# Copies of x moved from SyncE's queue to ScalarE's, and a reordered hand-over in a gated expert layer

## The chip, the cores and the metric

The kernel runs on one core of one Trainium2 chip. The metric is the device time of one execution in microseconds (us). The core has five engines, each with its own in-order instruction stream: TensorE (PE; its weight loads are shown apart as PEld), VectorE (DVE), ScalarE (ACT), GpSimd (POOL) and SyncE (SP, which here only begins DMAs). They meet through semaphores. DMAs begun by SyncE, ScalarE and GpSimd go through one queue each (q1, q10, q0 in the profile) and are carried out by the same 16 DMA engines.

## The reference

```python
W = weights[condition]                          # 64 of 16 matrices 64 x 64
y = einsum('bct,bcd->bdt', x, W)                # x: 64 x 64 x 1024, so 4096 rows ("tokens") of 1024
logits = y @ W_gate + b_gate                    # 8 experts
_, top_idx = top_k(logits, 2)
y_all = relu(einsum('bsd,edh->bseh', y, W_e) + b_e)   # W_e: 8 x 1024 x 1024
out = x + take_along_axis(y_all, top_idx[..., None], axis=2).mean(axis=2)
```

All is float32. Each token adds half of the relu of two experts' rows to its own row of x.

## The kernel before

**Two stages.** In the first, 32 tiles of 128 tokens are loaded, multiplied by their condition matrices on TensorE, copied from PSUM by ScalarE and stored in DRAM (y_rows); VectorE turns them for the gate. Tokens are dealt with in NG = 8 groups of 512 tokens. For group g VectorE chooses the two experts (choose), works out each token's place in its expert's list (slots), TensorE adds up the lists (fill) and VectorE writes them to SBUF (list_out). SyncE writes them to a table in DRAM, one slot per routed token, with eight small DMAs (table_out, L328).

In the second stage each tile is 128 slots of one expert: GpSimd gathers their rows of y (L471 for ordinary tiles, L457 for early ones), VectorE turns them, ScalarE casts them to a rounded high part (a_hi), VectorE subtracts it for the low part (a_lo), and TensorE does three products (high x high, high x low, low x high) at line 613, 48 matmul instructions a tile. VectorE adds the bias (finish, L1002), ScalarE does the relu (L731), and GpSimd adds the rows to out with a scatter that accumulates (L488 for early tiles, L500 for the others). There are 69 tiles.

**Early tiles.** Expert 0's first seven tiles (EARLY = 7, numbered 0 to 6) start before the table is complete: early tile t needs only tokens of the first t + 1 groups. SyncE reads its 128 slots back as soon as group t is in the table (read_first, L314, four DMAs), VectorE makes row numbers of them (read_from, L981), GpSimd gathers (early), VectorE turns (turn_early, L1018), ScalarE casts (early_hi, L737), VectorE subtracts (early_lo, L1023). TensorE does the products of early tiles 0 to 6 in order, with the gate work of groups 4 to 7 put between them by hand (hooks).

**From the table on.** Once all groups are in it, ScalarE loads the whole table to SBUF with four DMAs (L778), VectorE rearranges it in six kinds of instruction (L1096 to L1106) and makes the row numbers of all slots; GpSimd can then gather tile 7 and those after it, which are the ordinary tiles. schedule() works out which expert each tile belongs to. After the last early tile has been split (s_alo at EARLY) SyncE loads expert 1's bias and weights, which ScalarE and VectorE split into high and low parts (L726, L884).

**Copies.** out must hold x before results are added to it. The last four tiles are stored from SBUF; for the rest 14 copies of 1 MB go from x to out in DRAM (copy, L343), begun by SyncE and never more than two in flight: copy c waits for copy c - 2, with two semaphores in turn. scatter_early(t) waits for copies 2t and 2t + 1.

**What sets the order.** No planner does: every engine's stream is written out by hand. SyncE's tail reads: bias, copies 0 and 1, pad row block, table_out(4), copies 2 and 3, read_first(4), table_out(5), copy 4, read_first(5), copy 5, table_out(6), copy 6, read_first(6), copy 7, table_out(7), copies 8 to 13, and then bias and weights of expert 1. VectorE's tail is the straight list after its loop over 32 tiles, beginning with choose(LATE): it ends with read_from(6), schedule, early_out, finish_early(3), turn_early(5), early_lo(5), the table, finish_early(4), turn_early(6), early_lo(6), finish_early(5), and then tile 7.

Of the kernel before, what the change touches and what calls it, by code (L numbers as in the profile page):

```python
# [27 lines left out]
def build(nc, x, itok, cond_w, gate_w, gate_b, exp_w, exp_b, out, y_dram, table):  # L28
# [46 lines left out]
    with ExitStack() as ctx:  # L75
# [6 lines left out]
        def sem(name):  # L82
            return ctx.enter_context(nc.semaphore(name))
# [140 lines left out]
        s_copy = [sem(f"s_copy{i}") for i in range(2)]  # L224
# [74 lines left out]
        with nc.Block() as block:  # L299

            @block.sync
            def _(sp):
# [7 lines left out]
                def read_first(t):  # L310

                    sp.wait_ge(s_sc[t], LAND)
                    for q in range(Q):
                        sp.dma_start(first[q * R:(q + 1) * R, t, :], slots_by[:, t, :]).then_inc(s_first[t], 16)  # L314
# [24 lines left out]
                def copy(c):  # L339
                    if c >= 2:  # L340
                        sp.wait_ge(s_copy[c % 2], c // 2 * 16)
                    at = slice(left[c] * P, (left[c] + 2) * P)
                    sp.dma_start(out[at, :].rearrange("(o r) d -> r o d", o=2),  # L343
                                 x_rows[at, :].rearrange("(o r) d -> r o d", o=2)).then_inc(s_copy[c % 2], 16)

# [17 lines left out]
                sp.wait_ge(s_y, NTILE - 2)  # L363
                copy(0)
                copy(1)

                sp.dma_start(out[TOK:TOK + P, :], x_rows[0:P, :]).then_inc(s_pad, 16)
                table_out(LATE)
                copy(2)
                copy(3)  # L370
                read_first(4)
                table_out(LATE + 1)
                copy(4)
                read_first(5)
                copy(5)
                table_out(LATE + 2)
                copy(6)
                read_first(6)
                copy(7)
                table_out(LATE + 3)  # L380
                for c in range(8, len(left)):
                    copy(c)
# [26 lines left out]
            def _(pool):  # L409
# [70 lines left out]
                def scatter_early(t):  # L480

                    for j in range(2):
                        pool.wait_ge(s_copy[j], (t + 1) * 16)
                    if t:
                        pool.wait_ge(s_add, t * 16)
                    pool.wait_ge(s_out, t + 1)
                    pool.wait_ge(s_to, t + 1)
                    pool.indirect_dma_start(  # L488
                        out=out, out_offset=bass.IndirectOffsetOnAxis(ap=first_to[:, t:t + 1], axis=0),
                        in_=out_of(tile(0, t)), in_offset=None, compute_op=ALU.add).then_inc(s_add, 16)  # L490
# [193 lines left out]
            def _(act):  # L684
# [59 lines left out]

                conditions(0)
# [6 lines left out]
                for n in range(NTILE):  # L752
# [9 lines left out]
                    if n == NTILE - 4:  # L762
                        early_hi(0)
                early_hi(1)
                logits_out(NG - 2)
                relu(tile(0, 0))
                early_hi(2)
                logits_out(NG - 1)
                relu(tile(0, 1))
                early_hi(3)  # L770
                early_hi(4)
                relu(tile(0, 2))
                for g in range(NG):
                    act.wait_ge(s_sc[g], LAND)
                act.wait_ge(s_yout[0], 16 * NG)
                act.wait_ge(s_turn, NTILE)
                for q in range(Q):
                    act.dma_start(ys[q * R:(q + 1) * R, 0, :].rearrange("p (b w) -> p b w", w=P).bitcast(U32),  # L778
                                  slots_all).then_inc(s_tab, 16)
# [45 lines left out]
            def _(dve):  # L825
# [257 lines left out]
                turn_early(4)  # L1083
                early_lo(4)
                list_out(NG - 1)
                read_from(6)
# [4 lines left out]
                early_lo(5)  # L1091

# [17 lines left out]
                finish_early(4)  # L1110
                turn_early(6)
                early_lo(6)
# [83 lines left out]
```

## Time and profile before

| | us |
|---|---|
| median of 3 runs (lowest, highest) | 889.76 (889.64, 892.01) |
| the profiled execution | 886.84 |
| its span | 885.2 |
| PE busy | 849.0 (96%) |
| PEld busy | 672.8 (76%) |
| DVE busy | 428.8 (48%) |
| POOL busy | 447.3 (51%) |
| ACT busy | 257.0 (29%) |

The profile is of one execution; its times count from the start of its span. Busy shares are means over the whole span: the stretch in which the change lies is 100 to 210 us, where one stage hands over to the other. A row of a timeline gives start, length, engine, line, operation, written tile, read tiles, how many instructions are taken together, and in brackets the idle time of the engine before it and who ended it. Rows of SPq, ACTq and POOLq are the issuing of a DMA; the transfer itself comes after, and "landing" is the time from issue until all of it has arrived.

### The profile page before, as it was taken

To read this page: it belongs to the slowest core of one execution; us is meant where nothing else is said; L and a number is where in the kernel's file an instruction comes from. 1 tells how busy PE (TensorE), PEld (TensorE's weight loads), DVE (VectorE), ACT (ScalarE), POOL (GpSimd) and SP (SyncE) were. 2 spreads that over 40 slices of the span, in tenths; PEclk is the share of its full clock that TensorE was granted. 3 is DMA by queue.
4 is the path that set the end of the run, shared out by engine and by line. 5 is a ranking of instruction groups with operands and counts; after the bars stand their busy time and mean duration, and the time that the engine had idled before them with its cause. 6 is when DMAs were issued, how large, how long until landed. Compare 5 with 4: busy or idle time off the path is not lost.

```text
span 885.2 us, 16693 instructions
## 1 busy us (share of the span) xinstructions
PE 849.0 (96%) x4154; PEld 672.8 (76%) x4155; DVE 428.8 (48%) x578; ACT 257.0 (29%) x310; POOL 447.3 (51%) x500
## 2 busy tenths in 40 slices
PE   8788999899999999999999999999999999999993
PEld 4444577777888888888888888888888888888883
DVE  6698777656643373335533363336333733333320
ACT  5656411034421151114211331115111511111220
POOL 3002324267566667654665556555655465555311
PEclk9899999999999999999999999999999999999997
DMA  9999987998965695447754495546654565444433
GB/s 337 417 417 360 332 301 221 313 327 269 295 132 110 120 298 121 101 95 201 196 107 91 106 289 102 111 99 217 171 109 99 186 119 106 89 101 99 80 48 47
DMA packets 51034, 162.47 MB, mean 184 GB/s; under 512 B 11594, under 2 KB 11658, under 8 KB 50986
## 3 DMA queue, kind: packets, MB, share of 16 engines
q0 software_dynamic: 24544, 76.74, 40.0%
q1 hardware_dynamic: 20618, 67.79, 21.0%
q10 hardware_dynamic: 5840, 17.57, 5.0%
q8 instruction: 14, 0.23, 0.1%
q14 instruction: 18, 0.15, 0.0%
HBM read 106.74 MB, written 70.52 MB: 200 GB/s over the span
## 4 chain that ended last, share of the span: by engine, by line
PE 82%; DMA 6%; DVE 5%; issue 2%; ACT 2%; SPq 1%; ACTq 0%; POOL 0%; DVEq 0%; POOLq 0%
PE psO L613 79%; DMA y_rows<-ys 1%; DMA raw<-in_L_ffn_W_e 1%; DVE turned L864 1%; PE psO L554 1%; ACT ys L707 1%; DMA ys<-slot_table 1%; DMA first<-slot_table 1%; DMA slot_table<-lists 1%; DMA raw<-in_L_cond_weights 1%; SPq L328 1%; PE psG L566 0%; DVE w_lo L877 0%; DVE bias L1018 0%; SPq L325 0%
## 5 line engine op out<-in xcount | busy, mean ns | idle before, releaser
L613 PE MATMUL psO<-w_hi,a_hi 128*128 (+1 forms) x1104 | 342.6, 392 | 4.5 <-DVE a_lo L1023 3.5
L613 PE MATMUL psO<-w_hi,a_lo 128*128 (+1 forms) x1104 | 340.6, 390 | 0.0
L613 PE MATMUL psO<-w_lo,a_hi 128*128 (+1 forms) x1104 | 340.5, 390 | 0.0
L471 POOL DMA_INDIRECT rows<-y_rows,idx_g x248 | 255.5, 1030 | 106.7 <-issue 51.5
L613 PEld LDWEIGHTS psO<-w_hi,a_hi 128*128 128x128 f32 x1104 | 206.6, 188 | 49.3 <-DVE a_lo L1023 4.4
L613 PEld LDWEIGHTS psO<-w_lo,a_hi 128*128 128x128 f32 x1104 | 207.6, 188 | 43.3
L613 PEld LDWEIGHTS psO<-w_hi,a_lo 128*128 128x128 f32 x1104 | 207.6, 188 | 43.3
L1040 DVE TENSOR_TENSOR a_lo<-ys,a_hi 128x1024 fp32r<-128x1024 f32 x62 | 75.9, 1225 | 113.4 <-ACT a_hi L743 113.4
L731 ACT ACTIVATE ys<-ys 128x1024 f32<-128x1024 f32 x33 | 35.0, 1061 | 262.4 <-DVE ys L1002 262.4
L731 ACT ACTIVATE rows<-rows 128x1024 f32<-128x1024 f32 x33 | 35.0, 1060 | 249.7 <-DVE rows L1002 249.7
L1002 DVE TENSOR_TENSOR ys<-psO,bias 128x1024 f32<-128x1024 f32 x33 | 40.3, 1222 | 123.2 <-PE psO L613 91.9
L1002 DVE TENSOR_TENSOR rows<-psO,bias 128x1024 f32<-128x1024 f32 x33 | 40.4, 1223 | 112.4 <-PE psO L613 76.6
L1029 DVE STREAM_TRANSPOSE ys<-rows 128x1024 f32<-128x1024 f32 x62 | 76.7, 1237 | 14.1 <-DMA rows<-y_rows,idx_g 14.1
L884 DVE TENSOR_TENSOR w_lo<-raw,w_hi 128x1024 f32 x56 | 65.3, 1222 | 36.1 <-ACT w_hi L726 35.9
L500 POOL DMA_INDIRECT out<-rows,idx_s x31 | 55.2, 1781 | 40.2 <-issue 17.4
L500 POOL DMA_INDIRECT out<-ys,idx_s x31 | 53.6, 1730 | 37.7 <-ACT ys L731 18.3
L467 POOL COPY idx_g<-idx_all 128x4 uint32 x62 | 26.5, 427 | 87.3 <-issue 59.8
L743 ACT CAST a_hi<-ys 128x1024 fp32r<-128x1024 f32 x62 | 64.9, 1047 | 12.7 <-issue 9.8
L457 POOL DMA_INDIRECT raw<-y_rows,from_q x28 | 29.3, 1045 | 71.8 <-DVEq L982 51.3
L726 ACT CAST w_hi<-raw 128x1024 f32 x56 | 55.2, 1048 | 7.1 <-DMA raw<-in_L_ffn_W_e 5.9
L864 DVE STREAM_TRANSPOSE turned<-ys 128x1024 f32<-128x1024 f32 x32 | 39.4, 1239 | 14.0 <-ACT ys L707 11.9
L707 ACT COPY ys<-psO 128x1024 f32<-128x1024 f32 x32 | 32.4, 1012 | 21.0 <-PE psO L554 14.0
(141 smaller groups left out, 333.3 us busy)
## 6 DMA issues: line engine op xcount, KB each, us to landing
raw<-in_L_ffn_W_e SPq DMA_DIRECT2D x56, 512.0 KB, 5.9
y_rows<-ys ACTq DMA_DIRECT2D x32, 512.0 KB, 8.7
out<-in_x SPq DMA_DIRECT2D x14, 1024.0 KB, 6.4
rows<-in_x SPq DMA_DIRECT2D x16, 512.0 KB, 10.5
more_x<-in_x SPq DMA_DIRECT2D x16, 512.0 KB, 10.4
bias<-in_L_ffn_b_e SPq DMA_DIRECT2D x8, 512.0 KB, 7.1
rows<-y_rows,idx_g POOLq DMA_INDIRECT x248
raw<-in_L_ffn_W_e POOLq DMA_DIRECT2D x4, 512.0 KB, 9.1
```

What stands on the lines that cost most here:

```text
L471: pool.indirect_dma_start(out=rows[:, slot, a * DQ:(a + 1) * DQ], out_offset=None, in_=y_parts[0:(1 + TOK) * Q, :], in_offset=bass.Indirec ...
L500: pool.indirect_dma_start(out=out, out_offset=bass.IndirectOffsetOnAxis(ap=idx_s[:, m:m + 1], axis=0), in_=o_sb[m], in_offset=None, comput ...
L613: last = nc.tensor.matmul(ps[:, h * BANK:(h + 1) * BANK], a[:, p, k * P:(k + 1) * P], w[:, bass.ds(slot + (k * H + h * BANK), BANK)], star ...
L707: nc.scalar.copy(ys[:, s, :].rearrange("p (q k j) -> p q k j", q=Q, k=KD), psO[n % 2][:, :].rearrange("p (k q j) -> p q k j", q=Q, k=KD)). ...
L726: nc.scalar.copy(w_hi[:, bass.ds(at, H)], raw[:, k, :]).then_inc(s_hi, 1)
L731: nc.scalar.activation(out_of(t), out_of(t), ACTF.Relu, scale=0.5).then_inc(s_out, 1)
L743: nc.scalar.copy(a_hi[:, m % 2, :], ys[:, m % 2, :]).then_inc(s_ahi, 1)
L864: V.transpose(turned[:, g % 2, :, s * R:(s + 1) * R], ys[:, s, :].rearrange("p (b i) -> p b i", i=R)).then_inc(s_turn, 1)
L884: V.tensor_tensor(w_lo[:, bass.ds(at, H)], raw[:, k, :], w_hi[:, bass.ds(at, H)], ALU.subtract).then_inc(s_split, 1)
L1002: V.tensor_tensor(out_of(t), psO[m % 2][:, :], bias[:, bass.ds((e % 2) * H, H)], ALU.add).then_inc(s_bo, 1)
L1029: V.transpose(ys[:, p, :].rearrange("p (k a i) -> p k a i", k=KD, a=Q), rows[:, p, :].rearrange("p (a k j) -> p k a j", k=KD, a=Q)).then_i ...
L1040: V.tensor_tensor(a_lo[:, p, :], ys[:, p, :], a_hi[:, p, :], ALU.subtract).then_inc(s_alo, 1)
```

## The change

SyncE begins no copies any more, so nothing on it waits for one. It writes lists 4 to 7, reads the slots of early tiles 4 to 6 each after its own list, and then begins the load of the whole table in ScalarE's place. ScalarE begins all 14 copies in five batches between its other work, waits for none, and each copy has a semaphore of its own. On VectorE read_from(6) goes from behind list_out(7) to ahead of early_lo(4), and finish_early(4), turn_early(6), early_lo(6) go from behind the work on the table to ahead of the wait for it.

```diff
-        s_copy = [sem(f"s_copy{i}") for i in range(2)]
+        s_copy = [sem(f"s_copy{i}") for i in range((NTILE - G) // 2)]
@@ SyncE
-                def copy(c):
-                    if c >= 2:
-                        sp.wait_ge(s_copy[c % 2], c // 2 * 16)
-                    at = slice(left[c] * P, (left[c] + 2) * P)
-                    sp.dma_start(out[at, :].rearrange("(o r) d -> r o d", o=2),
-                                 x_rows[at, :].rearrange("(o r) d -> r o d", o=2)).then_inc(s_copy[c % 2], 16)
-
...
                 load_bias(0)
-                sp.wait_ge(s_y, NTILE - 2)
-                copy(0)
-                copy(1)
 
                 sp.dma_start(out[TOK:TOK + P, :], x_rows[0:P, :]).then_inc(s_pad, 16)
-                table_out(LATE)
-                copy(2)
-                copy(3)
-                read_first(4)
-                table_out(LATE + 1)
-                copy(4)
-                read_first(5)
-                copy(5)
-                table_out(LATE + 2)
-                copy(6)
-                read_first(6)
-                copy(7)
-                table_out(LATE + 3)
-                for c in range(8, len(left)):
-                    copy(c)
+                for g in range(LATE, NG - 1):
+                    table_out(g)
+                    read_first(g)
+                table_out(NG - 1)
+
+                for g in range(NG):
+                    sp.wait_ge(s_sc[g], LAND)
+                sp.wait_ge(s_yout[0], 16 * NG)
+                sp.wait_ge(s_turn, NTILE)
+                for q in range(Q):
+                    sp.dma_start(ys[q * R:(q + 1) * R, 0, :].rearrange("p (b w) -> p b w", w=P).bitcast(U32),
+                                 slots_all).then_inc(s_tab, 16)
                 sp.wait_ge(s_alo, EARLY)
@@ GpSimd
-                        pool.wait_ge(s_copy[j], (t + 1) * 16)
+                        pool.wait_ge(s_copy[2 * t + j], 16)
@@ ScalarE
+                def copies(lo, hi):
+
+                    for c in range(lo, hi):
+                        at = slice(left[c] * P, (left[c] + 2) * P)
+                        act.dma_start(out[at, :].rearrange("(o r) d -> r o d", o=2),
+                                      x_rows[at, :].rearrange("(o r) d -> r o d", o=2)).then_inc(s_copy[c], 16)
+
...
                         early_hi(0)
+                copies(0, 3)
                 early_hi(1)
                 logits_out(NG - 2)
+                copies(3, 5)
                 relu(tile(0, 0))
                 early_hi(2)
+                copies(5, 7)
                 logits_out(NG - 1)
+                copies(7, 9)
                 relu(tile(0, 1))
                 early_hi(3)
+                copies(9, 12)
                 early_hi(4)
                 relu(tile(0, 2))
-                for g in range(NG):
-                    act.wait_ge(s_sc[g], LAND)
-                act.wait_ge(s_yout[0], 16 * NG)
-                act.wait_ge(s_turn, NTILE)
-                for q in range(Q):
-                    act.dma_start(ys[q * R:(q + 1) * R, 0, :].rearrange("p (b w) -> p b w", w=P).bitcast(U32),
-                                  slots_all).then_inc(s_tab, 16)
+                copies(12, len(left))
                 relu(tile(0, 3))
@@ VectorE
                 turn_early(4)
+                read_from(6)
                 early_lo(4)
                 list_out(NG - 1)
-                read_from(6)
                 schedule()
                 early_out(4, EARLY)
                 finish_early(3)
                 turn_early(5)
                 early_lo(5)
+                finish_early(4)
+                turn_early(6)
+                early_lo(6)
 
                 dve.wait_ge(s_tab, Q * 16)
...
                 dve.sem_inc(s_idx, 1)
-                finish_early(4)
-                turn_early(6)
-                early_lo(6)
                 finish_early(5)
```

## Rows read from the trace of the kernel before

**Rows 1.** The page, part 5: product group, its busy time and waiting
```profile
L613 PE MATMUL psO<-w_hi,a_hi 128*128 (+1 forms) x1104 | 342.6, 392 | 4.5 <-DVE a_lo L1023 3.5
```

**Rows 2.** Chain that ended last, in order of time: start, length, what
```profile
207.08 109.09 PE psO L613 x480
316.31 555.18 PE psO L613 x2448
```

**Rows 3.** Timeline of TensorE, 150 to 215 us
```profile
167.22 0.61 PE L613 MATMUL psO<-w_hi,a_lo 128*128 128x512 f32 x2
170.53 0.73 PE L613 MATMUL psO<-w_hi,a_hi 128*128 128x512 f32 x2 [2.70 <-DVE a_lo L1023]
...
184.15 0.73 PE L613 MATMUL psO<-w_hi,a_hi 128*128 128x512 f32 x2 [0.81 <-DVE a_lo L1023]
...
195.17 0.61 PE L613 MATMUL psO<-w_hi,a_hi 128*128 x2
...
207.08 0.72 PE L613 MATMUL psO<-w_hi,a_hi 128*128 x2 [0.88 <-DVE a_lo L1040]
```

**Rows 4.** Windows: length, busy PE PEld DVE ACT POOL, PEclk, DMA share, GB/s
```profile
171.00:174.00 3.00, 3.00 (x11) 2.35 (x10) 1.26 (x2) 0.00 (x0) 0.00 (x0) 0.64 1.03 285
174.00:177.00 3.00, 3.00 (x12) 2.41 (x11) 2.79 (x4) 0.00 (x0) 0.00 (x0) 0.79 1.01 414
```

**Rows 5.** Timeline of VectorE, 95 to 215 us
```profile
152.81 1.23 DVE L1023 TENSOR_TENSOR a_lo<-bias,a_hi 128x1024 fp32r<-128x1024 f32 x1 [1.11 <-ACT a_hi L737]
...
154.30 0.21 DVE L947 TENSOR_TENSOR lists<-list_high,psL 64x64 uint32<-64x64 f32 x1
158.00 0.23 DVE L981 TENSOR_SCALAR from_q<-first,part_q 128x4 uint32<-128x4 uint32 x1 [3.49 <-DMA first<-slot_table]
...
169.25 1.22 DVE L1023 TENSOR_TENSOR a_lo<-bias,a_hi 128x1024 fp32r<-128x1024 f32 x1 [1.11 <-ACT a_hi L737]
172.71 1.11 DVE L1096 COPY ys<-ys 128x1024 uint32<-128x1024 uint32 x1 [2.23 <-DMA ys<-slot_table]
...
179.32 1.23 DVE L1002 TENSOR_TENSOR rows<-psO,bias 128x1024 f32<-128x1024 f32 x1 [0.22 <-DVE idx_row L996]
...
182.82 1.27 DVE L1023 TENSOR_TENSOR a_lo<-bias,a_hi 128x1024 fp32r<-128x1024 f32 x1 [1.12 <-ACT a_hi L737]
...
187.90 1.25 DVE L1029 STREAM_TRANSPOSE ys<-rows 128x1024 f32<-128x1024 f32 x1 [2.67 <-DMA rows<-y_rows,idx_g]
190.31 1.26 DVE L1040 TENSOR_TENSOR a_lo<-ys,a_hi 128x1024 fp32r<-128x1024 f32 x1 [1.16 <-ACT a_hi L743]
...
201.05 1.24 DVE L1029 STREAM_TRANSPOSE ys<-rows 128x1024 f32<-128x1024 f32 x1
...
205.46 1.23 DVE L1040 TENSOR_TENSOR a_lo<-ys,a_hi 128x1024 fp32r<-128x1024 f32 x1 [2.06 <-ACT a_hi L743]
```

**Rows 6.** Timeline of GpSimd: last of the four gathers for tile 7
```profile
182.48 0.95 POOL L471 DMA_INDIRECT rows<-y_rows,idx_g  x1 [0.30 <-issue]
```

**Rows 7.** Timeline of SyncE: the issuing of DMAs
```profile
148.71 0.58 SPq L343 DMA_DIRECT2D out<-in_x  x1
151.39 1.73 SPq L314 DMA_DIRECT2D first<-slot_table  x4
...
159.37 20.39 SPq L343 DMA_DIRECT2D out<-in_x  x6
```

**Rows 8.** Landing of read_first: all, then those issued 151 to 153.2 us
```profile
DMA to landing us min/median/max: 1.7/5.5/8.0
...
first<-slot_table SPq DMA_DIRECT2D x4, 0.5 KB, 4.5
```

**Rows 9.** Issue of DMAs: table load by ScalarE, and all copies by SyncE
```profile
162.38 1.77 ACTq L778 DMA_DIRECT2D ys<-slot_table  x4
...
L343 SPq DMA_DIRECT2D out<-in_x x14: 572/580/1832, 104.8 to 179.2; - x14
```

**Rows 10.** Timeline of ScalarE: cast of early tile 1
```profile
110.62 1.05 ACT L737 CAST a_hi<-bias 128x1024 fp32r<-128x1024 f32 x1 [5.31 <-DVE bias L1018]
```

## The prediction

> **What bounds the kernel now.** I read the page first. Its fifth part puts the three products of line 613 at some 343 us each and gives their engine 4.5 us of waiting in all, 3.5 of it for the low halves of early tiles (L1023) [rows 1]. The chain of waits then shows where it could move: from 207.08 us to 871.49 there is nothing but TensorE on the products [rows 2]. After 207 us TensorE never waits. So the question is only when the product of tile 8 (the second ordinary tile) starts, 207.08 now. An edit that moves this start moves the end by as much; one that doesn't is worth nothing.
>
> The TensorE timeline shows the holes ahead of it [rows 3]: 2.70 us before early tile 5 (170.53), 0.81 before early tile 6 (184.15), none before tile 7 (195.17), 0.88 before tile 8. After the hole of 2.70 us the granted clock is 0.64 in 171 to 174 and 0.79 in 174 to 177 [rows 4], the lower of the two levels (1.2 GHz) for part of each, while PE is fully busy. In work that is 3.0 x 0.36 + 3.0 x 0.21 = 1.7 us. The 0.8 us holes were followed by no fall. All that can be won is 2.70 + 1.7 + 0.81 + 0.88 = 6.1 us.
>
> Why they are there, by VectorE's timeline [rows 5]: it runs strictly in order. At 154.51 it has written list 7, then idles 3.49 us for the read of early tile 6's slots (158.00), then does schedule and turns early tile 5; its low half ends at 170.47, and TensorE starts 0.06 later. Then 2.23 us of waiting for the whole table (172.71), some 6.5 us of work on it, and only then tile 6.
>
> **The change part by part.**
> 1. read_from(6) moves ahead of early_lo(4) and list_out(7). This is the edit that speaks against the change: the instruction waits for a DMA, and behind it stand the low half of early tile 4, which TensorE wants at about 167.83 - 10.95 = 156.9 (the last product of tile 4 ends at 167.83, [rows 3], and a tile takes 184.15 to 195.17, some 11.0), and list 7, from which the table comes. Call F the moment at which the read of tile 6 is there: 158.00 now. The low half then ends at F + 0.35 + 1.23 and list 7 at F + 2.05, where both were done by 154.51.
> 2. All behind it on VectorE follows F. From 158.00 to the end of early tile 5's low half are 12.47 us [rows 5]; the two moved items add 154.51 - 152.81 = 1.70. So tile 5 starts at F + 12.47 + 1.70 + 0.06 = F + 14.2. Break-even against 170.53 is F = 156.3.
> 3. finish_early(4), turn_early(6), early_lo(6) come ahead of the table. They took 179.32 to 184.09 [rows 5], 4.8 us: tile 6 is ready at F + 19.0, while TensorE needs it only at F + 25.2. The 0.81 hole goes, for sure.
> 4. The price is paid by the table: its work starts at S = F + 19.0 instead of 172.71. From there to the end of tile 7's low half it took 191.57 - 172.71 = 18.86 [rows 5], so F + 37.8. In it lie 4.47 us between GpSimd's last gather issue (ends 183.43) and the turn (187.90) [rows 5, 6], beside the copies (issued to 179.76 [rows 7]); a small read was back in as little as 1.7 [rows 8]. I let it come between 2 and 4.5: F + 35.3 to F + 37.8. TensorE is there after two tiles, F + 14.2 + 22.0 = F + 36.2. Tile 7 so starts at F + 36.2 to F + 37.9; I take F + 36.6.
> 5. Bias and weights of expert 1 are begun by SyncE when early tile 6 is split (s_alo at 7), so at F + 19 instead of 184.1. The weights were the cause that VectorE turned tile 8 only at 201.05; from that turn to the end of the low half are 5.64 us [rows 5]. Now they lie ready: four splits of 1.2 us after tile 7's low half, the turn, and 5.64 come to some 10.5 to 11 us after it, against the 10.95 that tile 7 keeps TensorE busy. Hole 0 to 0.5, taken 0.2 instead of 0.88. **Tile 8 starts at F + 36.6 + 10.95 + 0.2 = F + 47.8**, against 207.08 now.
> 6. SyncE: table_out and read_first no longer stand behind copies' waits, and it begins the table's loads (four issues took ScalarE 1.77 us [rows 9]). It is idle otherwise. The table took 172.71 - 154.51 = 18.2 us from list to landing; S allows it F + 19.0 - (F + 2.05) = 17.0. It needs to be 1.2 us quicker, and the copies that ran beside it (six from 159.37 to 179.76 [rows 7]) are by then all begun: the last go out after relu of tile 2, some 154 to 157 us. I count it as in time; if it isn't, 1.2 us.
> 7. ScalarE issues 14 copies. One issue was 0.57 to 1.83 us on SyncE [rows 9]: at most 3 x 1.83 = 5.5 for the batch of three. The first batch stands ahead of 5.31 us of idle time before the cast of early tile 1 [rows 10]; the other batches stand ahead of such waits too. Cost 0; if the cover were gone in one place, 0.5 to 2 us, and it would have to be made up in front of list 4 to 7.
> 8. Separate semaphores: scatter_early(t) waits for the same copies as before, all of them earlier. 0.
>
> **What F is.** Before, the four reads are issued in 151.39 to 153.12, right behind a 1 MB copy issued on the same queue at 148.71 [rows 7], and their median landing is 4.5 us after issue [rows 8]. The issue time stays: it is set by TensorE's count for list 6 and the landing of its writes. After, no copy stands ahead in SyncE's queue, but up to three (begun at 141 or later) are in ScalarE's, and the adding scatter of early tile 1 in GpSimd's. Bounds for the landing from the reads' own row: 1.7 and 8.0, so F = 154.8 to 161.1. I take 157.3, near to the same read before (158.0) with a little off for the copy that no longer stands in front: the scatter remains.
>
> The Trainium skill (DMA: Bandwidth & Descriptors, section Queues, rings and completion order) says that each DMA engine takes the queues that have work for it in turn, a packet from each; by that the read passes a backlog in another queue. The same page, under Issuing engines are not separate DMA queues, says that starting DMAs from several engines saves only the issue time. By the first F would fall, by the second it would stay at 158.0 and the table would be no quicker. No row of before has such a read beside copies in the other queue alone; the second is a rival below.
>
> **Sum.** F = 157.3 gives a start of tile 8 at 205.1, 2.0 us sooner. The profiled execution took 886.84 us (span 885.2 and 1.6 around it), so 884.8 for such an execution; it lies 2.9 under the median of the runs, 889.76, so for a median 887.8. What a measurement here can tell from no change is about 0.3%, 2.7 us. By steps: hole 5 with its slow clock becomes a smaller hole before tile 4 (F + 1.7 - 156.9 = 2.1) and one of 1.5 before tile 5. Should the clock fall after the first, tile 4 runs 1.7 longer inside that second hole and nothing is lost; should it fall after the second, up to 1.4 is.
>
> **Rivals.**
> - *The read is back much sooner* (F = 154.8 to 156.6). For it: nothing in front on its queue, and a landing of 1.7 is on the row. Against: the scatter of 128 rows that stood beside it stays. At 155.3 tile 8 starts at 203.1: 4.0 won, 885.8. Bound 154.8: 885.3.
> - *Slower: the moved wait holds list 7.* The place is read_from(6) on VectorE. If the transfers are no quicker for being begun by another engine, F = 158.0 and the table is 1.2 late; its work then needs the full 18.86: list 7 at F + 2.05, table at F + 20.25, tile 7 at F + 39.2, tile 8 at F + 50.3 = 208.3, 1.2 slower, 891.0. Every us that the read comes later costs one more. (The second rule of the Trainium skill cited above would have it so.) With F = 161.1 it is 211.4, 4.3 slower, 894.1. It decides from F = 156.8 if the table is slow, and from F = 159.3 if it isn't. For it: DMA engines are busy all through 150 to 180. Against: the copies leave that stretch.
> - *A hidden wait takes the place*, nothing is gained: the hole before tile 5 turns into one before tile 7 of the same size (gathers land no sooner and the clock falls in tile 5): F + 38.0 + 10.95 + 0.5 = 206.8, 889.4.
>
> **How the numbers follow.** Forecast 0.40 (a tenth of it beyond 2.7 us), sooner read 0.28, slower rival 0.22 (nearly half beyond 2.7 us), hidden 0.10. So faster 0.32, same 0.58, slower 0.10. The range reaches from near the bound of the sooner read, 885.2, to 891.7, past the slower rival's 891.0; what is left out is about 0.08 below and 0.10 above. The forecast's own range is 886.7 to 889.3.
>
> **What would show it.** In the profile after: VectorE idle in front of from_q of tile 6, now ahead of the low half of early tile 4, until about 157.3; a new hole of TensorE of some 2 us before tile 4; a hole before tile 5 smaller than 2.70; none before tile 6; tile 6's low half ending about F + 19; the table's first instruction right behind with no wait for the DMA; tile 8 at about 205. Wrong would make it: a wait of VectorE for the table after tile 6, a read that needs over 6 us, a hole before tile 7 of more than 1.5 us, ScalarE late for a cast because of its issues, or waits of TensorE after 210 us.

## The result, and the profile after

| | before | changed |
|---|---|---|
| median of 3 runs, us (lowest, highest) | 889.76 (889.64, 892.01) | 903.04 (899.89, 905.02) |
| ratio, 95% interval | | 1.0137 [1.0084, 1.0189] |
| profiled execution, span | 886.84, 885.2 | 903.04, 901.4 |

Slower by about 12 us (the interval reaches from 7.5 to 16.8), where 2 us faster was forecast and the range ended at 891.7. The profile of before is of an execution 2.9 us below its median, that of the changed kernel is at its median, so the two profiles differ by more, 16.2 us. All ratios are of fast executions; of experiment 10 below one of five, which took 3971.69 us, is left out.

First the chain that ended last, in order of time, as in [rows 2]:

```profile
231.72 655.92 PE psO L600 x2880
887.91 1.24 DVE rows L995
```

TensorE is without a wait only from 231.72 on, and that is the start of tile 9 and not of tile 8. Line 600 is line 613 of before. The timeline of TensorE shows three holes where [rows 3] had 2.70, 0.81 and 0.88 us:

```profile
143.22 0.61 PE L573 MATMUL psR<-stack,LT 128*128 128x32 f32 x2 [4.79 <-DVEq L901]
...
170.91 1.22 PE L600 MATMUL psO<-w_hi,a_hi 128*128 128x512 f32 x2 [4.94 <-DVE a_lo L1016]
...
231.72 1.21 PE L600 MATMUL psO<-w_hi,a_hi 128*128 x2 [3.61 <-DVE a_lo L1033]
```

They stand in early tile 2 (a piece of gate work), before early tile 4 and before tile 9. VectorE's timeline tells why; compare [rows 5]:

```profile
140.75 0.23 DVE L974 TENSOR_SCALAR from_q<-first,part_q 128x4 uint32<-128x4 uint32 x1 [8.18 <-DMA first<-slot_table]
...
151.66 0.21 DVE L940 TENSOR_TENSOR lists<-list_high,psL 64x64 uint32<-64x64 f32 x1
...
169.26 0.23 DVE L974 TENSOR_SCALAR from_q<-first,part_q 128x4 uint32<-128x4 uint32 x1 [8.60 <-DMA first<-slot_table]
...
171.02 0.21 DVE L940 TENSOR_TENSOR lists<-list_high,psL 64x64 uint32<-64x64 f32 x1
...
188.20 1.23 DVE L1016 TENSOR_TENSOR a_lo<-bias,a_hi 128x1024 fp32r<-128x1024 f32 x1 [1.11 <-ACT a_hi L724]
189.34 1.07 DVE L1092 COPY ys<-ys 128x1024 uint32<-128x1024 uint32 x1
...
191.73 1.29 DVE L1096 TENSOR_SCALAR idx_all<-ys,part_q 128x1024 uint32<-128x1024 uint32 x1
...
219.92 1.25 DVE L1022 STREAM_TRANSPOSE ys<-rows 128x1024 f32<-128x1024 f32 x1 [3.96 <-DMA rows<-y_rows,idx_g]
...
230.10 1.22 DVE L1033 TENSOR_TENSOR a_lo<-ys,a_hi 128x1024 fp32r<-128x1024 f32 x1
```

The waits for read 4 and the row numbers (idx_all) in the kernel before, which [rows 5] leaves out:

```profile
133.02 0.23 DVE L981 TENSOR_SCALAR from_q<-first,part_q 128x4 uint32<-128x4 uint32 x1 [1.86 <-DMA first<-slot_table]
...
175.13 1.28 DVE L1100 TENSOR_SCALAR idx_all<-ys,part_q 128x1024 uint32<-128x1024 uint32 x1
```

VectorE waits 8.18 us for read 4 (before: 1.86) and 8.60 us for read 6, which now stands ahead of list 7. The row numbers of all slots (idx_all) are there at 193.02; before at 176.41. SyncE's timeline shows where the reads lost their time, compare [rows 7]:

```profile
121.29 3.56 SPq L328 DMA_DIRECT2D slot_table<-lists  x8
131.47 1.98 SPq L314 DMA_DIRECT2D first<-slot_table  x4
...
152.84 3.55 SPq L328 DMA_DIRECT2D slot_table<-lists  x8
162.28 1.78 SPq L314 DMA_DIRECT2D first<-slot_table  x4
```

In the kernel before:

```profile
119.89 3.58 SPq L328 DMA_DIRECT2D slot_table<-lists  x8
123.51 1.28 SPq L343 DMA_DIRECT2D out<-in_x  x2
124.84 2.72 SPq L314 DMA_DIRECT2D first<-slot_table  x4
```

The eight writes of list 4 (16 KB in all) are issued by 124.85, and read 4, which waits for their landing, begins at 131.47: 6.6 us. Before, the same step was over within 1.4 us (issued by 123.47, the read at 124.84), though two copies were issued between. List 6's writes are issued by 156.39 and read 6 begins at 162.28, 5.9 us. ScalarE's timeline shows what they met:

```profile
107.09 5.33 ACTq L736 DMA_DIRECT2D out<-in_x  x3
...
114.42 2.23 ACTq L736 DMA_DIRECT2D out<-in_x  x2
...
124.26 1.31 ACTq L736 DMA_DIRECT2D out<-in_x  x2
...
127.80 1.50 ACTq L736 DMA_DIRECT2D out<-in_x  x2
```

Nine copies are begun by 129.3, where SyncE had begun four. The windows of 120 to 140 us, before and then after (columns as in [rows 4]), show the DMA engines going from 0.56 busy to 1.01:

```profile
120.00:140.00 20.00, 20.00 (x164) 15.68 (x163) 15.58 (x51) 3.55 (x5) 4.70 (x5) 1.00 0.56 182
```
```profile
120.00:140.00 20.00, 18.43 (x155) 14.04 (x153) 10.65 (x36) 2.38 (x3) 0.00 (x0) 1.00 1.01 333
```

After each of the three holes the granted clock is at the lower level for a while, longer than in [rows 4]. Windows of the changed kernel:

```profile
142.00:146.00 4.00, 2.78 (x8) 2.39 (x9) 3.43 (x12) 1.06 (x1) 3.09 (x4) 0.52 1.01 300
146.00:150.00 4.00, 4.00 (x18) 2.92 (x18) 3.55 (x15) 1.05 (x1) 2.28 (x2) 0.63 0.84 217
...
172.00:175.00 3.00, 3.00 (x9) 2.32 (x8) 2.69 (x12) 0.00 (x0) 2.38 (x3) 0.50 0.35 98
...
234.00:237.00 3.00, 3.00 (x8) 2.31 (x7) 1.12 (x1) 3.00 (x4) 1.43 (x1) 0.50 1.11 362
237.00:240.00 3.00, 3.00 (x13) 2.46 (x12) 3.00 (x4) 2.44 (x3) 0.00 (x0) 0.88 0.99 229
```

**The account.** List 7 is written at 171.23 instead of 154.51, 16.7 us later: 1.4 that this execution's early tiles began later, 6.3 that read 4 kept back list 6 (7.7 late at 151.87, less the 1.4), 3.5 more from list 6 to read 6 (17.4 us instead of 13.9), and 5.5 by the new order (list 7 ends 1.97 after read 6 is there instead of 3.49 before). The row numbers are 16.6 later. From them to the start of tile 9 it is 38.7 us (193.02 to 231.72): gathers of tiles 7 and 8, the scatter of early tile 3, the gather of tile 9, and what VectorE and ScalarE do behind each. In the kernel before the same 38.7 would end at 215.1, but TensorE came to tile 9 only at 207.08 + 10.95 = 218.0. By this estimate 2.9 us of slack are used up and tile 9 starts 13.7 later. The length of the chain is borne out by experiments 7, 12 and 15 (39.3, 39.5 and 39.0); in the kernel before itself tile 9's low half was ready somewhat later than that, at 216.98, with expert 1's weights split just ahead of it:

```profile
215.76 1.22 DVE L1040 TENSOR_TENSOR a_lo<-ys,a_hi 128x1024 fp32r<-128x1024 f32 x1
```

From tile 9 to the last product TensorE takes 655.92 us; in the kernel before it takes 871.49 - 218.03 = 653.46. These 2.5 us I put down to the lower clock after the hole, with no wait left to hide it. 13.7 and 2.5 are the 16.2 of the two profiles.

### The profile page after: what moved, and what is told of

Read it like the earlier page. It is cut to its first block, busy times and chain, and to the rows that moved or that the text cites. A ratio compares the mean times of both kernels' runs of the same rounds, so it can differ in the third digit from the quotient of the medians.

```text
span 901.4 us, 16693 instructions
## 1 busy us (share of the span) xinstructions
PE 855.8 (95%) x4154; PEld 678.1 (75%) x4155; DVE 428.5 (48%) x578; ACT 256.3 (28%) x310; POOL 447.7 (50%) x500
## 4 chain that ended last, share of the span: by engine, by line
PE 76%; DMA 8%; DVE 7%; issue 3%; ACT 2%; SPq 2%; POOL 1%; ACTq 0%; DVEq 0%; POOLq 0%
PE psO L600 74%; DMA first<-slot_table 2%; DMA slot_table<-lists 2%; PE psO L541 2%; DMA y_rows<-ys 1%; DVE turned L857 1%; ACT ys L694 1%; POOL rows L458 1%; SPq L328 1%; DMA out<-ys,first_to 1%; DMA rows<-y_rows,idx_g 1%; DMA raw<-in_L_cond_weights 1%; DVE bias L1011 1%; SPq L314 0%; SPq L325 0%
## 5 line engine op out<-in xcount | busy, mean ns | idle before, releaser
L857 DVE STREAM_TRANSPOSE turned<-ys 128x1024 f32<-128x1024 f32 x32 | 39.4, 1240 | 14.4 <-ACT ys L694 12.4
## 6 DMA issues: line engine op xcount, KB each, us to landing
out<-in_x ACTq DMA_DIRECT2D x14, 1024.0 KB, 17.9
```

The lines of the kernel that those rows point to most:

```text
L857: V.transpose(turned[:, g % 2, :, s * R:(s + 1) * R], ys[:, s, :].rearrange("p (b i) -> p b i", i=R)).then_inc(s_turn, 1)
```

## The experiments

Ratios are to the kernel before, timed on the same chip at the same time, with 95% intervals. In these timings the kernel before had medians of 890.1 to 892.7 us, so absolute times of traces can be compared with those of the kernel before only to some 3 us. "Row numbers" is the time at which those of all slots are ready.

**1. VectorE's order alone** (kernel before):

```diff
                 turn_early(4)
+                read_from(6)
                 early_lo(4)
                 list_out(NG - 1)
-                read_from(6)
...
                 early_lo(5)
+                finish_early(4)
+                turn_early(6)
+                early_lo(6)
...
-                finish_early(4)
-                turn_early(6)
-                early_lo(6)
```

> The kernel before with only VectorE's reorder (read of tile 6 ahead of list 7, tile 6 ahead of the table); the copies stay with SyncE. Backlog theory (the small list writes and slot reads meet megabytes of copies already begun; the reorder costs little): within 2 us of before, since the read of tile 6 is back at 158 as before; by my sum the start of tile 8 is 206 to 208, so 0.998 to 1.002 of before. Order theory (the moved wait for the read costs the most): 5 us or more slower, 1.006 or more.

1.0023 [1.0000, 1.0046]. Timelines of VectorE and TensorE:

```profile
160.33 0.23 DVE L981 TENSOR_SCALAR from_q<-first,part_q 128x4 uint32<-128x4 uint32 x1 [7.54 <-DMA first<-slot_table]
...
197.78 1.25 DVE L1029 STREAM_TRANSPOSE ys<-rows 128x1024 f32<-128x1024 f32 x1 [9.70 <-DMA rows<-y_rows,idx_g]
```
```profile
161.99 1.22 PE L613 MATMUL psO<-w_hi,a_hi 128*128 128x512 f32 x2 [3.89 <-DVE a_lo L1023]
...
201.83 1.21 PE L613 MATMUL psO<-w_hi,a_hi 128*128 x2 [4.57 <-DVE a_lo L1040]
...
216.26 0.73 PE L613 MATMUL psO<-w_hi,a_hi 128*128 x2 [0.43 <-DVE a_lo L1040]
```

The order costs some 2 us by itself, though the interval reaches down to nothing; the order theory's 5 us or more is excluded. The gather of tile 7 took 6.8 us to land (issued by 190.96) beside copies and expert 1's weights, begun at 190; I had forecast 2 to 4.5.

**2. The DMA part alone** (changed kernel, VectorE's order of before, experiment 1's edit undone).

> The changed kernel with VectorE in the order of before: only who begins which DMA, and when, is changed. Backlog theory: the first slot read after the loop is waited for some 8 us as in the changed kernel, and the time is 8 us or more above before (1.009 or more), nearly all of the loss. Order theory: within 3 us of before (1.003 or less).

1.0055 [1.0035, 1.0075]: read 4 waited for 7.14 us, row numbers at 183.87. Neither theory's number: 5 us, and with experiment 1's 2 us not the 12 of both. By the medians the parts add to less than the whole (0.8% of 1.4%), but the difference is no larger than what the intervals leave open.

**3. The same copies in SyncE's own queue** (changed kernel):

```diff
-                for g in range(LATE, NG - 1):
-                    table_out(g)
-                    read_first(g)
-                table_out(NG - 1)
+                sp.wait_ge(s_y, NTILE)
+                copies(0, 5)
+                table_out(LATE)
+                copies(5, 9)
+                read_first(LATE)
...
+                copies(9, 12)
+                table_out(LATE + 2)
+                read_first(LATE + 2)
+                copies(12, len(left))
+                table_out(NG - 1)
```

> The changed kernel with the same copies begun in the same places of the sequence (5 ahead of list 4, 4 ahead of read 4, 3 ahead of list 6, 2 ahead of list 7), but by SyncE, so all in one queue, the small transfers behind the copies. If it is the other queue that starves the small transfers, this is faster than the changed kernel, by 4 us or more. If it is the bytes begun ahead of them, it is as slow or slower: behind 5 copies list 4 waits some 10 us, read 4 behind 4 more about 10 us; 5 to 20 us slower than the changed kernel (910 to 925).

1.0158 [1.0118, 1.0198]; read 4 was waited for 16.66 us:

```profile
150.35 0.23 DVE L976 TENSOR_SCALAR from_q<-first,part_q 128x4 uint32<-128x4 uint32 x1 [16.66 <-DMA first<-slot_table]
```

ScalarE's queue is thus not what starves the small transfers: with the copies in the same queue the wait is twice as long. In part that is SyncE's own issuing (the last four copies took it 4.4 us, and read 4 began at 137.25 instead of 131.47), in part the read itself (there 13.1 us after its first issue instead of 9.3). The bytes begun ahead are what the two versions have in common.

**4. ScalarE's copies paced** (changed kernel):

```diff
-                copies(0, 3)
+                copies(0, 2)
...
+                act.wait_ge(s_sc[4], LAND)
+                copies(2, 4)
...
+                act.wait_ge(s_sc[5], LAND)
+                copies(4, 5)
...
+                act.wait_ge(s_tab, Q * 16)
+                copies(8, 10)
                 relu(tile(0, 4))
+                copies(10, len(left))
```

> The changed kernel with ScalarE's copies paced: each begun only when the small transfer that it would meet has landed (2 before list 4, 2 after it has landed, 1 after list 5, 1 after read 5, 1 after list 6, 1 after read 6, 6 after the table is loaded). Same queue as in the changed kernel, little backlog. Backlog theory: the loss goes, 13 to 17 us faster than the changed kernel, 886 to 890, 0.996 to 1.000 of before. Queue theory: still 5 us or more above before. Order theory: the same as the changed kernel to 3 us.

1.0086 [1.0054, 1.0118]. Read 4 was waited for 1.26 us, so that part held:

```profile
133.37 0.23 DVE L982 TENSOR_SCALAR from_q<-first,part_q 128x4 uint32<-128x4 uint32 x1 [1.26 <-DMA first<-slot_table]
```

But reads 5 and 6 were waited for 3.22 and 6.02 us, and the six copies that I had put behind the table met the gather of tile 7, for which VectorE waited 10.16 us. TensorE had holes of 4.95 us before early tile 4 and 6.61 before tile 7, and two later ones (1.56 at 241.08, 3.62 at 266.74). The expected end, 886 to 890, was missed; the number is the queue theory's. What speaks against that theory is experiment 3 and the wait for read 4 here: bytes moved out of one small transfer's way stood in another's.

**5 and 6. Reads ahead of copies in SyncE's queue** (kernel before), and with early tile 6 ahead of the table:

```diff
                 table_out(LATE)
+                read_first(4)
                 copy(2)
                 copy(3)
-                read_first(4)
                 table_out(LATE + 1)
-                copy(4)
                 read_first(5)
+                copy(4)
                 copy(5)
+                copy(6)
                 table_out(LATE + 2)
-                copy(6)
                 read_first(6)
```

> The kernel before (SyncE begins the copies, VectorE's order of before), with each slot read of early tiles 4 to 6 begun ahead of the copies that stood ahead of it, and one copy more brought into the stretch ahead of list 6. Backlog theory (a small transfer is as late as the copies begun ahead of it make it): VectorE's wait for read 6 falls from 3.49 to about 2 us, early tile 5 and the end come 1 to 3 us sooner, 0.997 to 0.999 of before. If the scatter with its additions is what holds read 6: no change, 1.000.

> The same, with early tile 6 turned ahead of the wait for the table (the one part of the change to VectorE's order that leaves list 7 ahead of read 6). My chain: tile 6's hole of 0.81 us goes and weights of expert 1 come earlier, the table's work is up to 2 us later: 1 to 4 us faster than before, 0.996 to 0.999. Rival: the weights' transfers, begun 8 us sooner, meet the gather of tile 7, which takes 7 us instead of 4.5 to land (as in the run with VectorE's reorder alone), and a hole of 3 us or more opens ahead of tile 7: 1.000 to 1.004.

The versions also drop the wait of copies 2 to 8 for the copy two before, and begin copy 8 ahead of list 7.

1.0030 [1.0000, 1.0060] and 1.0046 [1.0025, 1.0067]. Read 4's wait fell to 0.52 us, but with three copies begun ahead of list 6 its writes took 8.2 us to land (issued by 150.42, read 6 begun at 158.66), and read 6 came later still (161.59, waited for 6.21). In experiment 5 a hole of 8.42 us stood before early tile 5 and one of 2.12 before early tile 6; in experiment 6 one of 8.30 before early tile 5. Both expectations missed. Experiment 6 is near the rival's number but not by its way: the gather of tile 7 was waited for 5.73 us, yet before tile 7 there was a hole of only 0.25.

**7 and 12. Changed kernel with list 7 first** (its read_from(6) put back behind list_out(7)), and with early tile 5 too ahead of read 6:

> The changed kernel with one line moved back: list 7 is written ahead of the wait for read 6; tile 6 still ahead of the table. The wait moved ahead of list 7 costs 5.4 us of list 7 by the traces (3.49 that it waited after it, 1.97 of work). If it is worth that in the end: 4 to 7 us faster than the changed kernel, 1.005 to 1.009 of before, since the backlog stays. If the order is worth nothing beside the backlog: 1.012 or more.

> The changed kernel with VectorE in the order of the previous run (list 7, early tile 5, read 6, schedule, early tile 6); the copies as in the changed kernel. It parts the two losses: VectorE no longer keeps anything behind read 6, but read 4 (waited for some 8 us) still delays list 6 and list 7. Backlog theory: read 4's 8 us stay, 5 to 8 us slower than before, 1.005 to 1.009. If the order alone was the loss: 1.003 or less.

1.0102 [1.0073, 1.0130] and 1.0102 [1.0084, 1.0120]: by the medians some 3 us below the changed kernel, which the intervals don't part from it, with list 7 some 8 us earlier. Both lie above the range that I had expected (1.005 to 1.009), though their intervals reach into it. In experiment 7 list 7 came 8.1 us sooner and the row numbers only 3.5, since read 6 and early tile 6 still stand ahead of the table. Row numbers at 189.55 and 185.33, tile 9 at 228.81 and 224.87 after a hole of 1.72 and 4.60: 39.3 and 39.5 us behind them.

**8. Holes filled** (changed kernel): 60 small matmuls ahead of each of two waits.

```diff
+                def idle(count):
+                    for _ in range(count):
+                        nc.tensor.matmul(psX[:, 0:P], ones, before, start=True, stop=True)
```

> The changed kernel with 60 small matmuls into an unused bank ahead of each of TensorE's two long waits (4.8 us in early tile 2, 4.9 us ahead of early tile 4); they change no data and move no wait. Clock theory (about half of the loss is the granted clock, at its lower level for 6.8 us after each hole): no fall after the two holes, 3 to 7 us faster than the changed kernel, 1.006 to 1.010 of before. If the holes alone are the loss: as the changed kernel, 1.012 to 1.015.

1.0174 [1.0113, 1.0234]: not faster, so the clock theory's number missed. The first fill ended too early:

```profile
138.14 3.52 PE L629 MATMUL psX<-raw 128*128 128x128 bf16 x60
144.10 0.60 PE L573 MATMUL psR<-stack,LT 128*128 128x32 f32 x2 [2.44 <-DVEq L906]
```

2.44 us were left behind it, and the granted clock was 0.50 from 144 to 150 all the same. After the second hole, of which 1.24 us were left, the clock no longer fell, yet tile 9 started at 231.54, against 231.72. What TensorE saves ahead of a wait set elsewhere is given back in it.

**9 and 10. Kernel before, early tile 5 ahead of read 6 and schedule**; then tile 6 ahead of the table as well, whose load SyncE begins:

```diff
                 list_out(NG - 1)
-                read_from(6)
-                schedule()
-                early_out(4, EARLY)
                 finish_early(3)
                 turn_early(5)
                 early_lo(5)
+                read_from(6)
+                schedule()
+                early_out(4, EARLY)
```

> The kernel before with one edit on VectorE: early tile 5 (finish, turn, low half) goes ahead of the wait for read 6 and of schedule; list 7 stays first of all. If what costs is what stands behind a wait for a DMA on VectorE, the hole of 2.7 us before early tile 5 and its slow clock go, but tile 6 still waits for the table, so much of it comes back there: 0 to 3 us faster than before, 0.997 to 1.000. If the table-to-gather chain alone sets the end: no change, 1.000.

> The same, with early tile 6 too ahead of the table, and SyncE begins the table's load (ahead of copies 8 to 13 in its own queue), so that ScalarE waits for nothing there. Early tiles 5 and 6 then have no holes; the table's work starts at about 174 instead of 172.7 and its load is in sooner. 2 to 5 us faster than before, 0.994 to 0.998. Rival as for the run with tile 6 ahead: the weights meet the gather of tile 7, a hole of 4 us or more opens there, and it is no faster than before: 1.000 to 1.004.

1.0021 [1.0008, 1.0034] and 1.0033 [1.0004, 1.0063]. Both forecasts missed; in experiment 10 the rival came, in number and place. All holes were gathered in one: 7.49 us before early tile 6 in the first, 9.38 us before tile 7 in the second.

**11. ScalarE paced anew, VectorE's order of experiment 12.**

> ScalarE begins the copies, paced by the landing of lists and reads and spread behind the table (2, 2, 1, 2, 1, 2, 4), SyncE the rest, VectorE: list 7 first, then early tile 5, then read 6, schedule and early tile 6. Backlog theory: read 4 is waited for under 2 us, and it is within 3 us of before on either side, 0.997 to 1.003. Queue theory (copies in ScalarE's queue always delay the small transfers of SyncE): 1.006 or more.

1.0094 [1.0071, 1.0117], with read 4 waited for 1.11 us, a hole of 3.60 us before early tile 6 and one of 7.06 before tile 7: VectorE waited 8.08 us for its gather. Missed like experiment 4, with the queue theory's number again.

**13 and 14. The fill where the hole is the last, and where it is not.** Experiment 9 with 30 matmuls of 512 columns ahead of early tile 6; the kernel before with 10 ahead of early tile 5.

```diff
                 early_products(5)
+                idle(30)
                 early_products(6)
```

> The run with early tile 5 ahead of read 6, with 30 matmuls of 512 columns (6.8 us by the products' 0.227 us each) into an unused bank ahead of early tile 6, where that run had one hole of 7.49 us and then the lower clock for 6.8 us with no wait after it. Clock theory (the fall costs where no later wait hides it): 2 to 4 us faster than that run (1.0021), so 0.997 to 1.000 of before. If the chain on VectorE hides it here too: 1.001 to 1.003.

> The kernel before with 10 such matmuls (2.3 us) ahead of early tile 5, in the hole of 2.70 us after which the clock fell for 3.4 us. By both theories the fall is hidden here, since early tile 6 waits for VectorE until 184 anyway: within 0.15% of before. If the clock's fall were paid in full: 1.7 us faster, 0.998.

0.9981 [0.9966, 0.9997] and 1.0001 [0.9982, 1.0019]. Windows of experiment 9, then of 13:

```profile
184.00:188.00 4.00, 0.82 (x2) 0.73 (x3) 2.89 (x3) 1.72 (x2) 2.65 (x4) 0.50 0.86 336
188.00:192.00 4.00, 4.00 (x14) 3.14 (x14) 2.39 (x3) 2.10 (x2) 3.09 (x4) 0.71 0.94 254
```
```profile
184.00:188.00 4.00, 4.00 (x19) 3.16 (x19) 2.88 (x3) 1.96 (x2) 2.78 (x4) 1.00 0.93 344
188.00:192.00 4.00, 4.00 (x19) 3.33 (x18) 2.48 (x3) 2.11 (x2) 2.91 (x4) 1.00 0.80 249
```

The two differ in the filling matmuls alone, and 1.0021 becomes 0.9981, 3.6 us; with the two intervals it is 2 to 5. The traces show less: from early tile 6 to the last product experiment 9 took 687.8 us (187.18 to 874.98), and experiment 16 below, with no fall there, 686.1 (179.48 to 865.56) for the same 63 tiles. So 1.7 us of clock are seen, and the rest is open. Both expectations came true. In experiment 14 the hole was not gone but moved: none before early tile 5, 3.31 us before early tile 6 with a short fall behind it (0.67 and 0.76 in 188 to 194). Experiment 13 is the only complete version that beat the kernel before.

**15 and 16. Copies cut to a sixteenth**, in the changed kernel and in the one before:

```diff
-                        at = slice(left[c] * P, (left[c] + 2) * P)
+                        at = slice(left[c] * P, left[c] * P + 16)
```

The other rows of out don't get x here, so these two are measurements and no versions to use.

> The changed kernel with each copy cut to 16 of its 256 rows (the other rows of out never get x), so that hardly any bytes are in flight. Backlog theory: read 4 is not waited for, read 6 is back by 157, and it is near my forecast for the order, 885 to 890 where before has 890 (0.994 to 1.000). If the order on VectorE and the gathers after the table were the loss: 1.005 or more still.

> The kernel before with the copies cut in the same way: what the copies cost there. Backlog theory: they were placed behind the small transfers and cost little, mostly in front of read 6 and beside the table's load: 2 to 5 us faster than before (0.994 to 0.998). The difference between this and the previous run is what the rest of the change is worth when no copy is in the way.

0.9964 [0.9948, 0.9980], inside the expected range, and 0.9912 [0.9887, 0.9937], below it: the copies cost the kernel before some 8 us, and I had expected 2 to 5. VectorE and TensorE in experiment 15:

```profile
153.41 0.23 DVE L974 TENSOR_SCALAR from_q<-first,part_q 128x4 uint32<-128x4 uint32 x1 [0.86 <-DMA first<-slot_table]
```
```profile
216.02 1.22 PE L600 MATMUL psO<-w_hi,a_hi 128*128 x2 [3.84 <-DVE a_lo L1033]
```

Read 6 is back at 153.41, better than my lower bound, and still there is a hole of 3.84 us before tile 9, 39.0 us behind the row numbers (177.06). In experiment 16 they are ready at 171.7, tile 9's low half ends 39.4 behind them, 1.2 ahead of TensorE, and the only hole after early tile 0 is one of 0.87. So the copies cost the changed kernel 1.0137 / 0.9964 = 1.7% and the kernel before 0.9%; by the medians that is 7 to 8 us of the 12. The other 0.5%, 4 to 5 us, is there with no copy in the way. Where it arises the two traces show; list 7 and the table's first instruction, experiment 15, then 16:

```profile
155.17 0.21 DVE L940 TENSOR_TENSOR lists<-list_high,psL 64x64 uint32<-64x64 f32 x1
...
173.41 1.07 DVE L1092 COPY ys<-ys 128x1024 uint32<-128x1024 uint32 x1
```
```profile
154.19 0.21 DVE L947 TENSOR_TENSOR lists<-list_high,psL 64x64 uint32<-64x64 f32 x1
...
168.04 1.09 DVE L1096 COPY ys<-ys 128x1024 uint32<-128x1024 uint32 x1 [1.01 <-DMA ys<-slot_table]
```

List 7 is 1.0 us later in experiment 15, and from there to the table's work it is 4.4 us more: early tile 6 stands between. With no copy in the way it is thus early tile 6 ahead of the table, and hardly the moved wait, that makes the row numbers late. With whole copies the same stretch took as long in both kernels (18.1 and 18.2 us), since in the kernel before VectorE had to wait for the table until then. That the order on VectorE is the cause of the 4 to 5 us is my reading of these traces; the order alone wasn't run without copies.

## Why the prediction was wrong, point by point

- **What bounds the kernel** held: the end follows the last hole of TensorE. That the start of tile 8 decides did not: the last hole moved to tile 9, at 231.72, which the prediction had named as a sign of being wrong (a wait of TensorE after 210 us).
- **F, the moment of read 6**, was the step that failed most: 157.3 taken, 154.8 to 161.1 as bounds, 169.26 measured. "The issue time stays" was wrong (162.28 instead of 151.39). I asked only what the copies do to read 6, and not to list 4, read 4 and list 6 before it. Experiments 3 and 4 show them to be the cause (16.66, 8.18 and 1.26 us of waiting for read 4 with nine copies in its own queue, nine in the other, four paced), and in experiment 15, with hardly any bytes in the copies, read 6 is there at 153.41. The row that should have warned me is in the windows of before: DMA engines 0.56 busy in 120 to 140. The prediction doesn't look at that stretch; the idle share there went with quick small transfers, and the changed kernel used it up.
- **The landing itself**: the range of 1.7 to 8.0 nearly held for the slot reads (1.5 to 8.3 over all, 5.5 for read 6). Missing was that the writes of a list can take as long (6.6 us for list 4, 5.9 for list 6), and that every read stands behind its list's writes.
- **The moved wait** (F + 2.05 for list 7, break-even at 156.3) was priced rightly: list 7 was there at F + 1.97.
- **Tile 6 ahead of the table**: its hole went, as forecast, and the table's work followed with no wait (189.34). The sum F + 47.8 for tile 8 came out: tile 9 at 231.72 less its hole of 3.61 and a tile of 10.9 is 217.2, F + 48.0. Two terms of it were off and made up for each other: tile 6's low half ended at F + 20.2 instead of F + 19.0, since VectorE waited 1.12 us for TensorE's tile 4, and the gather of tile 7 was there 1.8 us after its last issue, just under my lower bound. In experiment 1 the same gather took 6.8 us, and tile 8 started at F + 55.9 (216.26, with F = 160.33). So that the sum held in the changed kernel is in part luck.
- **The term that was missing** is the next step: gather 9 behind gathers 7 and 8 and a scatter on GpSimd, some 39 us from the row numbers to the start of tile 9. I put it at nothing without looking. With it later row numbers had a price beyond 2.9 us, the hole of 3.61 us before tile 9 and the lower clock behind it. Experiment 15 shows this with no copies: F is early and tile 9 waits.
- **The clock**: I put 1.7 us in what can be won and called a fall in front of a later wait hidden. The second hole of experiment 8 and experiment 14 bear out the hiding, 13 the price where nothing hides it. The three holes of before add up to 4.4 us, and only the first made the clock fall.
- **ScalarE's issues** took 1.78 us each in the first batch (forecast at most 1.83), and the cast of early tile 1 started 1.8 us later than before, 1.4 of it because this execution's early tiles began later. The other 0.4 is ScalarE's batch, 5.33 us long where 5.31 were idle before; VectorE didn't wait for it.
- **Queues.** Read 4 was waited for 8.18 us with the copies in another queue and 16.66 with them in its own, and both versions were slower than the kernel before. The Trainium skill (DMA: Bandwidth & Descriptors, Queues, rings and completion order) says that engines take queues in turn. The trace agrees as far as the shorter wait goes, but taking turns didn't make the read quick. By the same page, Issuing engines are not separate DMA queues, another engine saves only issue time. The runs bear it out in that the other engine won nothing; beside issue time the read itself was quicker too (9.3 against 13.1 us). I gave this rival 0.22 and priced it with an unchanged backlog.
- **Rivals**: the slower one had the right place (read_from(6) ahead of list 7). Its line of one us for each us gives 891.0 + 169.26 - 158.0 = 902.3, and 903.04 was measured; but it had tile 8 at F + 50.3 with the table late. The table wasn't late, tile 8 came at F + 48.0, and tile 9's hole, which it lacked, filled the difference. The nearness is chance.

**The steps that failed**, in short: "the issue time stays" (read 6 issued 10.9 us later, F = 169.26 for 157.3), and "tile 8 decides" (tile 9's gather chain put at nothing, 3.6 us of hole and 2.5 of clock).

Left open: how much of the 5 us of experiment 2 is read 4 and how much is copies beside other gathers. The halves of the change weren't tried without copies.

## What to carry to other kernels

A DMA engine that looks idle between two bulk transfers may be what makes a chain of small dependent transfers quick; before bulk is begun earlier, follow every small transfer that it will meet, from the first on. A wait put ahead of the item that starts the longest chain delays the whole chain, but what that costs in the end depends on the slack behind it (in experiment 7 list 7 came 8.1 us sooner and the row numbers 3.5). Holes of TensorE add up to what the chain on another engine sets, so closing one opens the next, and a single long one cost more than several short ones (1.0021 in experiment 9), since the clock fell after it; work on it pays only for the last.

## What the runs showed of the hardware

- With nine 1 MB copies begun in 22 us, a copy took 17.9 us to land (median of all 14; 6.4 before), and writes of 2 KB in another queue 6.6 us instead of at most 1.4.
- The granted clock in the 3 us after a hole of TensorE, with TensorE at work on the products: 1.00 after holes of 0.8 to 2.12 us; 0.70 after that of 2.70 (kernel before, 170.6 to 173.6) and 0.72 after one of 3.31 (experiment 14); after unfilled holes of 3.6 us and more 0.50 in most cases and never above 0.65.
- With matmuls into an unused bank up to the end of the hole the clock stayed at 1.00 (experiment 13); where they ended 2.44 us too early it was 0.50 for 6 us (experiment 8).
